# Another order of rounds in the last, quantized feed-forward stage

## The reference, cut to what matters

```
def bitlinear(x, w, b):
    dqx = act_quant_fake(x)       # per row: round(x * s) / s, s = 127 / max|x|, held to -128..127
    dqw = weight_quant_fake(w)    # round(w * s) held to -1..1, / s, s = 1 / mean|w|
    return einsum('btd,hd->bth', dqx, dqw) + b

h = layernorm(x, ln1_g, ln1_b)
h = bitlinear(h, w1, b1)          # 256 -> 1024
h = gelu(h)
h = layernorm(h, ln2_g, ln2_b)
h = bitlinear(h, w2, b2)          # 1024 -> 256
x = x + tanh(g_ffn[3]) * h
```

## Time and profile before

| | |
|---|---|
| Median of three runs | 1442.02 us (1438.07 to 1448.39) |
| The profiled execution's own time | 1443.31 us |
| Its span, first to last instruction | 1441.6 us |
| Last stage, from 1345.7 us to the end | 95.9 us |
| Busy in the last stage | PE 57.4, ACT 57.0, DVE 54.2, POOL 28.3 us |
| Mean granted TensorE clock, whole span and last stage | 0.92 and 0.73 of full speed |

### The profile page before, as it was taken

One profiled execution on the slowest core, in us unless ns is written; L12 is line 12 of the kernel. 1 busy time (PEld: TensorE's weight loads), 2 busy tenths in 40 slices (PEclk: granted clock), 3 DMA queues, 4 the chain that ended last, 5 costly groups with the idle time before them and its releaser, 6 DMA issues. The chain is left out here.

```text
span 1441.6 us, 25435 instructions
## 1 busy us (share of the span) xinstructions
PE 1206.0 (84%) x9539; PEld 948.0 (66%) x9539; DVE 859.9 (60%) x1950; ACT 686.2 (48%) x1533; POOL 538.8 (37%) x538
## 2 busy tenths in 40 slices
PE   2999999999996797589999379999998079999665
PEld 2677777777774365457776378988888057777333
DVE  6664565555443246667776646666674367777474
ACT  3345543454442222256666145445552047766465
POOL 3355554555553000288887431011100440450232
PEclk9999999999997998889999579999999579999886
DMA  6000000000001151300110445556650250000000
GB/s 174 6 7 12 12 1 12 12 1 1 1 1 22 30 153 33 88 21 22 42 32 2 172 150 172 198 187 194 187 177 17 80 164 23 23 2 2 1 10 17
DMA packets 59929, 88.63 MB, mean 61 GB/s; under 512 B 8640, under 2 KB 49808, under 8 KB 59808
## 3 DMA queue, kind: packets, MB, share of 16 engines
q1 hardware_dynamic: 57696, 81.49, 18.6%
q0 software_dynamic: 2112, 5.51, 1.3%
HBM read 81.48 MB, written 5.51 MB: 60 GB/s over the span
## 5 line engine op out<-in xcount | busy, mean ns | idle before, releaser
L906 POOL TENSOR_SCALAR a_arena<-a_arena 112x487 f32<-112x487 f32 x128 | 193.0, 1519 | 176.5 <-DVE a_arena L1117 176.5
L1198 ACT ACTIVATE a_arena<-banks,a_arena 112x487 f32<-112x487 f32 x128 | 84.3, 663 | 192.3 <-DVE a_arena L1111 192.3
L1111 DVE TENSOR_REDUCE a_arena<-banks 112x2 f32<-112x974 f32 x64 | 75.0, 1172 | 102.7 <-PE banks L997 102.7
L93 PE MATMUL banks<-f_x_high,f_up_high 128*128 128x256 f32 x448 | 128.3, 286 | 3.6 <-DVE f_up_low L1981 2.2
L94 PE MATMUL banks<-f_x_low,f_up_high 128*128 128x256 f32 x448 | 127.9, 286 | 0.0
L95 PE MATMUL banks<-f_x_high,f_up_low 128*128 128x256 f32 x448 | 127.8, 285 | 0.0
L397 POOL TENSOR_TENSOR a_arena<-a_arena 112x375 f32<-112x375 f32 x128 | 114.9, 925 | 24.1 <-ACT a_arena L704 23.9
L513 PE MATMUL banks<-ident,a_arena 112*126 112x112 f32 x768 | 105.8, 275 | 12.0 <-POOL a_arena L397 9.5
L513 PEld LDWEIGHTS banks<-ident,a_arena 112*126 112x126 f32 x768 | 77.6, 144 | 46.4 <-issue 26.8
L2018 POOL DMA_INDIRECT f_arena<-f_rows,f_arena x28 | 32.1, 1146 | 194.5 <-PE banks L2051 175.0
L2162 DVE TENSOR_TENSOR f_arena<-banks,f_arena 128x512 f32<-128x512 f32 x56 | 38.4, 686 | 100.4 <-ACT f_arena L2141 100.4
(11 more groups left out here) (333 smaller groups left out, 3326.6 us busy)
## 6 DMA issues: line engine op xcount, KB each, us to landing
f_arena<-in_L_ffn_w1T SPq DMA_DIRECT2D x14, 1024.0 KB, 6.1
f_arena<-in_L_ffn_w3T SPq DMA_DIRECT2D x14, 1024.0 KB, 5.0
f_arena<-in_L_ffn_w2T SPq DMA_DIRECT2D x14, 1024.0 KB, 5.7
a_arena<-in_ctxT SPq DMA_DIRECT2D x24, 375.0 KB, 5.1
a_arena<-in_ctx SPq DMA_DIRECT2D x16, 375.0 KB
f_y<-f_arena SPq DMA_DIRECT2D x14, 256.0 KB, 5.0
a_arena<-in_L_xattn_Wkv SPq DMA_DIRECT2D x2, 1024.0 KB, 9.9
a_arena<-in_fside_BxSxS SPq DMA_DIRECT2D x8, 164.1 KB, 2.4
```

The costliest lines, as they stand in the source:

```text
L93: pe.matmul(out, sh, mh, start=start, stop=False)
L906: pool.tensor_scalar(z, z, inv[:, n % 4, s:s + 1], None, ALU.mult).then_inc(p_ready, 1)
L1111: dve.tensor_reduce(negmax[:, n % 4, :], banks[0:T, 0:2, 0:KEYS], AX, ALU.max, negate=True).then_inc(max_ready, 1)
L1198: act.activation(prob[n % PR][s][:, 0:KEYS], banks[0:T, s, 0:KEYS], ACT.Exp, bias=negmax[:, n % 4, s:s + 1], accum_out=total[:, n % 4, s:s ...
```

## The change

It keeps every step's arithmetic and changes the following in the last stage.

- ScalarE's second rounding pass goes, for the rows and for the hidden values. The constant stays in, the values are turned in fp32, and the copy out of PSUM becomes an Identity activation that subtracts the constant and writes bf16.
- For that psZ takes two banks and psY one; `down(b)` waits for `add(b-1)`.
- VectorE runs three `rows` ahead, `centre` is split in `variance` and `centre`, and round b is rows(b+3), variance(b), centre(b), mean(b+1), scaled(b), add(b-1).
- ScalarE's round b is whole_rows(b+2), whole_hidden(b-1), gelu(b+1), move_rows(b+2), move_hidden(b-1), square_hidden(b+1).
- TensorE's round b is turn_rows(b+2), the bias product of b+2 (`up_bias`), turn_hidden(b-1), up(b+2), down(b-1).
- GpSimd makes the first diagonal of b+2 ahead of power(b).
- The constants are set by GpSimd in the attention before, a bf16 identity is no longer made, and ScalarE runs one two element wide Gelu at the stage's start.

```diff
@@ QuantizedWeights
     def tensor(self, pe, ps):
-        pe.wait_ge(self.made, 1)
+        pe.wait_ge(self.made, 3)
...
     def gpsimd_ones(self, pool):
         pool.memset(self.ones, 1.0).then_inc(self.made, 1)
+        pool.memset(self.shift[:, 0:1], ROUND).then_inc(self.made, 1)
+        pool.memset(self.shift[:, 1:2], -ROUND).then_inc(self.made, 1)
@@ quantized_ffn
-        psX = m.ps("psX").bitcast(BF16)[:, 0:DC * T].rearrange("p (c t) -> p c t", t=T)
-        psZ = m.ps("psZ").bitcast(BF16)[:, 0:HC * T].rearrange("p (c t) -> p c t", t=T)
-        psY = [m.ps(f"psY{j}") for j in range(2)]
+        psX = m.ps("psX")[:, 0:DC * T].rearrange("p (c t) -> p c t", t=T)
+        psZ = m.ps("psZ", 2)[:, :, 0:HC // 2 * T].rearrange("p k (c t) -> p k c t", t=T)
+        psY = m.ps("psY")
@@ gpsimd
             norm.gpsimd_power(pool)
-            pool.memset(shift[:, 0:1], ROUND).then_inc(made, 1)
-            pool.memset(shift[:, 1:2], -ROUND).then_inc(made, 1)
-            pool.tensor_copy(identb, ident[:]).then_inc(made, 1)
             diagonal(diag1, undo1, 0, h_undone, h_diag, u_ready)
             diagonal(diag1, undo1, 1, h_undone, h_diag, u_ready)
             for b in range(B):
-                power(b)
                 if b + 2 < B:
                     diagonal(diag1, undo1, b + 2, h_undone, h_diag, u_ready)
+                power(b)
                 diagonal(diag2, undo2, b, z_undone, z_diag, y_ready)
@@ tensor
-                    mm = pe.transpose(psX[:, c, :], hB[b % 2][:, c * P:(c + 1) * P], identb[0:T, 0:T])
+                    mm = pe.transpose(psX[:, c, :], h[:, b, c * P:(c + 1) * P], ident[0:T, 0:T])
...
-                    mm = pe.transpose(psZ[:, c, :], zq[b % 2][:, c * P:(c + 1) * P], identb[0:T, 0:T])
+                    mm = pe.transpose(psZ[:, c // (HC // 2), c % (HC // 2), :], z[b % 3][:, c * P:(c + 1) * P],
+                                      ident[0:T, 0:T])
...
             for b in range(2):
                 turn_rows(b)
+                up_bias(b)
                 up(b)
-            for b in range(B):
+            for b in range(B + 1):
                 if b + 2 < B:
                     turn_rows(b + 2)
+                    up_bias(b + 2)
+                if b:
+                    turn_hidden(b - 1)
+                if b + 2 < B:
                     up(b + 2)
-                turn_hidden(b)
-                down(b)
+                if b:
+                    down(b - 1)
@@ scalar
-                act.activation(hh, hh, ACT.Identity, bias=shift[0:T, 0:1], scale=scale1[:, b:b + 1]).then_inc(h_shifted, 1)
-                act.wait_ge(h_shifted, b + 1)
-                if b > 1:
-                    act.wait_ge(h_turned, b - 1)
-                act.activation(hB[b % 2], hh, ACT.Identity, bias=shift[0:T, 1:2]).then_inc(h_whole, 1)
+                act.activation(hh, hh, ACT.Identity, bias=shift[0:T, 0:1], scale=scale1[:, b:b + 1]).then_inc(h_whole, 1)
...
-                act.copy(hT[b % 2], psX).then_inc(h_moved, 1)
+                act.activation(hT[b % 2], psX, ACT.Identity, bias=shift[:, 1:2]).then_inc(h_moved, 1)
...
                 act.activation(z[b % 3], z[b % 3], ACT.Identity, bias=shift[0:T, 0:1], scale=scale2[:, b:b + 1]
-                               ).then_inc(z_shifted, 1)
-                act.wait_ge(z_shifted, b + 1)
-                if b > 1:
-                    act.wait_ge(z_turned, b - 1)
-                act.activation(zq[b % 2], z[b % 3], ACT.Identity, bias=shift[0:T, 1:2]).then_inc(z_whole, 1)
+                               ).then_inc(z_whole, 1)
...
-                act.copy(zT[b % 2], psZ).then_inc(z_moved, 1)
-            act.wait_ge(made, 3)
+                act.activation(zT[b % 2].rearrange("p (k c) t -> p k c t", k=2), psZ, ACT.Identity, bias=shift[:, 1:2]
+                               ).then_inc(z_moved, 1)
+            act.wait_ge(qw.made, 3)
+            act.activation(warm, shift, ACT.Gelu)
             for b in range(2):
                 whole_rows(b)
                 move_rows(b)
             gelu(0)
             square_hidden(0)
-            gelu(1)
-            for b in range(B):
+            for b in range(B + 1):
                 if b + 2 < B:
                     whole_rows(b + 2)
+                if b:
+                    whole_hidden(b - 1)
+                if b + 1 < B:
+                    gelu(b + 1)
+                if b + 2 < B:
                     move_rows(b + 2)
-                whole_hidden(b)
+                if b:
+                    move_hidden(b - 1)
                 if b + 1 < B:
                     square_hidden(b + 1)
-                move_hidden(b)
-                if b + 2 < B:
-                    gelu(b + 2)
@@ vector
-            rows(0)
-            rows(1)
+            for b in range(3):
+                rows(b)
             mean(0)
             for b in range(B):
+                if b + 3 < B:
+                    rows(b + 3)
+                variance(b)
                 centre(b)
-                if b + 2 < B:
-                    rows(b + 2)
-                scaled(b)
                 if b + 1 < B:
                     mean(b + 1)
+                scaled(b)
                 if b:
                     add(b - 1)
             add(B - 1)
```

More of the change, by code:

```diff
@@ L2224, in __init__ @@
         self.slab = SLAB
-        m = Memory(nc, ctx, dict(st, semaphores=[]), "qw", words=3 * SLAB + 3 * HID + 3 * D + P + 40, side="right")
+        m = Memory(nc, ctx, dict(st, semaphores=[]), "qw", words=3 * SLAB + 3 * HID + 3 * D + P + 44, side="right")
         self.w = [m.sb("w1", [P, SLAB]), m.sb("w2", [P, SLAB])]
@@ L2231, in __init__ @@
         self.total, self.mean, self.scale = (m.sb(n, [P, 2]) for n in ("total", "mean", "scale"))
-        self.gained = m.sb("gained", [P, 1])
+        self.gained, self.shift = m.sb("gained", [P, 1]), m.sb("shift", [P, 2])
         self.w_loaded, self.v_loaded, self.made, self.summed = (m.sem(n) for n in (
@@ L2306, in quantized_ffn @@
         h = norm.xn
-        identb = m.sb("identb", [P, P], BF16)
-        shift = m.sb("shift", [P, 2])
-        hB = [m.sb(f"hB{u}", [T, D], BF16) for u in range(2)]
+        shift, warm = qw.shift, m.sb("warm", [P, 2])
         hT = [m.sb(f"hT{u}", [P, DC, T], BF16) for u in range(2)]
-        z, zq = [m.sb(f"z{u}", [T, HID]) for u in range(3)], [m.sb(f"zq{u}", [T, HID], BF16) for u in range(2)]
+        z = [m.sb(f"z{u}", [T, HID]) for u in range(3)]
         zT, square = [m.sb(f"zT{u}", [P, HC, T], BF16) for u in range(2)], m.sb("square", [T, HID])
@@ L2317, in quantized_ffn @@
         psU = [m.ps(f"psU{j}", 2) for j in range(2)]
[L2318 to L2323 removed]
+        psX = m.ps("psX")[:, 0:DC * T].rearrange("p (c t) -> p c t", t=T)
+        psZ = m.ps("psZ", 2)[:, :, 0:HC // 2 * T].rearrange("p k (c t) -> p k c t", t=T)
+        psY = m.ps("psY")
+        h_step, h_ready, h_undone, h_whole, h_turned, h_moved, h_diag = (m.sem(n) for n in (
+            "h_step", "h_ready", "h_undone", "h_whole", "h_turned", "h_moved", "h_diag"))
         u_ready, gelu_done, mean_made, squared, ve_made, rstd_made = (m.sem(n) for n in (
             "u_ready", "gelu_done", "mean_made", "squared", "ve_made", "rstd_made"))
[L2326 to L2327 removed]
+        z_step, z_ready, z_undone, z_whole, z_turned, z_moved, z_diag = (m.sem(n) for n in (
+            "z_step", "z_ready", "z_undone", "z_whole", "z_turned", "z_moved", "z_diag"))
         y_ready, y_added, stored = m.sem("y_ready"), m.sem("y_added"), m.sem("stored")
@@ L2369, in turn_rows, with up_bias @@
                 for c in range(DC):
-                    mm = pe.transpose(psX[:, c, :], hB[b % 2][:, c * P:(c + 1) * P], identb[0:T, 0:T])
+                    mm = pe.transpose(psX[:, c, :], h[:, b, c * P:(c + 1) * P], ident[0:T, 0:T])
                 mm.then_inc(h_turned, 1)
-            def up(b):
+            def up_bias(b):
                 pe.wait_ge(h_diag, b + 1)
@@ L2380, in up @@
                               start=True, stop=False)
+            def up(b):
                 pe.wait_ge(h_moved, b + 1)
@@ L2398, in down @@
                 pe.wait_ge(z_diag, b + 1)
-                if b > 1:
-                    pe.wait_ge(y_added, b - 1)
-                pe.matmul(psY[b % 2][0:T, 0:D], diag2[b % 2], qw.b2, start=True, stop=False)
+                if b:
+                    pe.wait_ge(y_added, b)
+                pe.matmul(psY[0:T, 0:D], diag2[b % 2], qw.b2, start=True, stop=False)
                 pe.wait_ge(z_moved, b + 1)
                 for c in range(HC):
-                    mm = pe.matmul(psY[b % 2][0:T, 0:D], zT[b % 2][:, c, :], q2[:, c, :],
+                    mm = pe.matmul(psY[0:T, 0:D], zT[b % 2][:, c, :], q2[:, c, :],
                                    start=False, stop=(c == HC - 1))
                 mm.then_inc(y_ready, 1)
-            pe.wait_ge(made, 3)
             pe.wait_ge(qw.v_loaded, 96)
@@ L2511, in mean, with variance @@
```

(7 more changed lines are left out.)

4 lines of the change are left out of this document (2 added, 2 removed).

## The result

| | before | after |
|---|---|---|
| Median of four runs each | 1445.20 us (1438.07 to 1457.86) | 1427.82 us (1423.97 to 1433.60) |
| Profiled execution: time, span | 1443.31, 1441.6 us | 1423.97, 1422.2 us |
| Ahead of the last stage (to the start of VectorE's L183) | 1345.7 us | 1351.1 us |
| Last stage (from there to the end) | 95.9 us | 71.1 us |

The ratio of after to before is 0.9884, with a 95% interval of 0.9837 to 0.9932: faster by 1.2%. The span fell by 19.4 us while the stage that was changed fell by 24.8; the 5.4 us between them were lost ahead of it, in stages that the change does not touch. The other kernels put these down to scatter (see r1).

The account below looks back on a forecast made before the run. No engine full; the order of rounds sets the pace, VectorE waiting for ScalarE's squares. -2.4 - 10.0 - 9.9 - 0.1 + 3.5 = -18.9 us: profiled time 1424.4, median 1423 us, own range 1417 to 1427, outer 1415 to 1434.

Parts of the forecast that it names:

- The bound and the wait that goes: VectorE's rounds with `rows`: 2.99 us of idle for ScalarE's squares goes, 9.88 to 7.37 us, 10.0 us gained over four.
- The sum of row distances: VectorE's round with `rows`, added up from its pieces: 1.80 + 2.01 + 3.08 + 0.48 = 7.37 us.
- The last three steps: Between the last z_ready signals: 5.6 us each, 16.8 in all, so 9.9 us gained.
- 44.6 us of work predicted: ScalarE's work in the last stage, from 57.0 us, or 5.6 us a round, below VectorE's 7.37.
- TensorE at the high clock: TensorE's work per round at clock 1.00: 5.81 us, so it follows; eight fp32 turns in it 1.05 us.
- The start: Start of the last stage up to the first z_ready, which was to come at 1363.7 us, 2.4 us earlier.
- The tail: After the last z_ready: shorter by the pass, longer by turns and move, together -0.1 us.
- The clock: TensorE high in the middle, low at the start and in the last three rounds; one low round charged, 3.5 us.
- TensorE's full round of 10.86 us: TensorE's work in one round at the low clock, claimed to set the pace there instead of VectorE's 7.37 us.
- Nothing on the path needs it there: TensorE's turn_hidden(b-1), queued behind the bias, starts at 3.4 instead of 1.3 us after z_ready(b-1), claimed to cost no wait.
- The other cover I named: down(b-1) on TensorE waits for add(b-2) at the one psY bank; VectorE did that a round before, cover half a round.
- The rival of a late power: GpSimd's two diagonals need 3.06 us, so power comes 0.6 late eight times: 4.8 us, 1428 us; chance 0.08.

Follow-up runs that it names:

- r1: The changed kernel run again with no edit; last stage 75.6 us, ratio to the kernel before 0.9844.
- e3: The changed kernel with both rounding passes and bf16 turns put back; last stage 77.1 us, ratio to the kernel before 0.9886.
- e4: The changed kernel with GpSimd's old order, power(b) ahead of the first diagonal of b+2; last stage 93.5 us.
- e6: The changed kernel with rows(b+3) behind centre(b) instead of ahead of variance(b); last stage 80.4 us.
- e1: The kernel before with only one two element wide Gelu added at the start of the last stage; last stage 93.7 us.

## Why the prediction was right, point by point

The forecast was -18.9 us for the profiled execution, and its span fell by 19.4. That match is partly luck. The stage fell by 24.8, in r1 by 20.3, and the stages ahead happened to cost 5.4. The median came to 1427.82 us for the 1423 of the forecast, just above the 1427 at which its own range ended and inside the outer one of 1415 to 1434; the kernel before came out 3.2 us above the 1442.0 that it started from.

- **The bound and the wait that goes.** Right. VectorE's 2.99 us for the squares left every round, and its own queue became the bound, 7.37 us predicted and 7.28 measured. The sum of row distances was 0.09 too long per round, in add. e3 shows that this is the order's work: it keeps both passes and has the 7.28.
- **The last three steps.** 16.8 predicted, 16.95 in after, 19.5 in r1.
- **ScalarE.** 44.6 us of work predicted, 44.2 measured, again with some luck. The sum takes off the 1.28 of the table load, which moved to the start of the stage and is still in it; without that slip it is 45.9. The move took 1.01 for my 1.03, the small one 0.45 for 0.48.
- **TensorE at the high clock.** Eight turns took 0.93 for my 1.05 (at the low clock 1.70 to 1.76 for 1.84).
- **The start.** -2.4 predicted, -3.8 in after and -2.4 in r1. Of the 1.4 between the two, 1.3 is the clock in the first bias and `up`, 3.32 and 1.03 against 3.71 and 1.91 us.
- **The tail.** -0.1 predicted, -0.5 in after and -1.1 in r1, by the clock and the turns.
- **The clock.** I charged 3.5 us for one low round in all. After held nearly none in the steps, r1 two. Taken without this charge the forecast is -22.4, between r1 and after. The size was right, the mechanism was not: I had TensorE's full round of 10.86 us set the pace. In fact a bias product behind an idle time ran low and ended 1.7 us later, and what it delayed was down(b-1). The step that failed is "Nothing on the path needs it there: y_ready(b-1) is asked for only after scaled(b)". That is when add(b-1) asks, and it had to wait 1.19 and 2.96 us in r1's two long steps and 0.55 in after. The other cover I named, half a round for down(b-1) at the one psY bank, held: no down product waited for an add in after or r1.
- **GpSimd.** The rival of a late power did not occur: both diagonals beside 256 wide passes took 1.11 together (1.27 in the first round), not 3.06. I gave the early diagonal no price, since moving the bias needed no wait. e4 shows that the other order costs 22 us: I costed this edit at nothing, and without it nine tenths of the gain are gone. The rival's mechanism is at work on the diagonals instead of on power, in e6 and ahead of r1's sixth step, where the wide pass meets them.
- **Edit by edit.** Order with GpSimd's swap: 95.9 to 77.1 (e3, table load included). Second pass out: 77.1 to 75.6 (r1) or 71.1 (after). Table load: 2.2 alone (e1). They do not add up: the second pass was worth 7.7 us alone and 1.5 behind the order, since VectorE then no longer waits for the squares behind it.

What stays open: what decides in which round the clock falls. Two executions of the same kernel differ in it by 4.5 us of stage, and with the same 2.76 us of idle ahead of it the same product ran at the high level in one and at the low one in the other. Which stages ahead scatter by 14 us, and why, was not tried.

## What to carry to other kernels

Give the pace of a stage as one engine's queue, piece by piece, and then ask of every instruction in that queue what it waits for if the others run at their slow level: the add that was "asked for late" was the next bound. An engine that is busy a third of the time can still hold most of the gain in the order of two of its instructions; follow its queue as a ring, not its busy time. When fillers and reorderings are weighed, read the stage from the profile, as the rest of a long program scatters by more than the change.

## What the runs showed of the hardware

- In GpSimd a pair of 112 x 112 diagonals took 1.11 us beside 256 wide passes of VectorE and 1.98 to 2.50 beside a 1024 wide pass with two operands. The Trainium skill ("SBUF — State Buffer", Who interferes with whom) has VectorE contend with a GpSimd instruction that reads SBUF when its own two inputs lie there, and the first to start hold the pair of ports for the whole instruction. The 2.50 fits that. Beside the narrow passes little of such a cost shows: in after one diagonal took 0.57 to 0.73 us there and two took 1.11 to 1.27.
- fp32 turns of 112 x 128 cost 0.36 us more per eight than bf16 ones at the high clock (0.93 against 0.57, the latter at 1388.36 in the kernel before), and 0.77 to 0.83 more at the low one (1.70 to 1.76 against 0.93).
- Twelve products of 512 columns, with no result that anyone reads, brought the first bias from 3.32 us to 1.97. The granted clock over that bias (1355.9 to 1358.0) was 1.00, the high level of 2.4 GHz, where it was 0.57 over the bias in after (1354.9 to 1358.2).
